# Attention with the softmax division moved behind the value product, in a 16-sequence attention and expert kernel

## The chip, the cores and the metric

The kernel runs on one core of a Trainium2 chip. The metric is the device time of one execution in microseconds; the median of three executions is taken. A core has five engines that run their own instruction lists and meet at semaphores: TensorE (PE in the profile), VectorE (DVE), ScalarE (ACT), GpSimd (POOL) and SyncE (SP, used here only to start DMAs). On-chip data lies in SBUF; TensorE writes its results to PSUM, which has 8 banks of 512 fp32 columns for each partition.

## What is computed

The input is 16 sequences of 256 tokens with 128 features. The reference, cut to its core:

```python
x = x + attention(layernorm(x))      # 16 heads of 64, 16 sequences of 256 tokens
x = x + experts(layernorm(x))        # 160 experts of 64, 8 chosen for each token, plus a shared one

# attention
dot = einsum('bihd,bkhd->bhik', q, k)
w = softmax(dot / sqrt(64), axis=-1)
a = einsum('bhij,bjhd->bihd', w, v)
return a.reshape(b, s, 1024) @ Wo + bo
```

## The kernel before

The kernel has three stages. The first does attention for all sequences, the choice of experts, and a scatter of each token's features into the slots of its 8 experts. The second does the shared expert and waits for the last scatters. The third streams the slots through the experts' weights and gathers the results. The change is in the first stage alone.

The first stage is a software pipeline. A step is one pair of heads of one sequence: 16 sequences times 8 pairs are 128 steps. In the code `b` is the sequence of the step that enters, `g` (0 to 7) its pair of heads, `step = 8 b + g`, and `u` is the step that an operation belongs to. `live(b, g, lag)` says whether the operation of step `u = step - lag` exists. Sequences 0 to 3 and the three that drain the pipeline are written out; 4 to 15 are a hardware loop over `b`. Each engine runs its own list in program order. In each step:

- TensorE does, in this order: scores of step u = step - 1 (line 379, into bank pair `psS`, three products of split fp32), queries and keys of this step (line 368, `psY`), attention output of step - 3 (line 414, `psO`, columns 0 to 255), in even `g` the values (line 368, `psVM`), transposes of the probabilities of step - 2 (line 429, `psT`, 8 blocks of 128 x 128), and the output projection of step - 4 (line 441, `psA`). Once in each sequence there are two transposes and the router's product (lines 455, 461, 499), and the ranks of the chosen experts (lines 486 to 493).
- ScalarE copies `qk_hi` (line 619), takes the exponential of the scores with their row sums in `rowsum` (line 627, four instructions in a step), copies `v_sb` in even `g` (line 633), copies the transposed probabilities of step - 2 (`probs_transposed`, line 270, two instructions), and multiplies one quarter of the probabilities of step - 1 by the inverse row sum (line 641).
- VectorE takes the row maxima (`negmax`, line 1055, two instructions), subtracts for `qk_lo` (line 1060), copies the attention output out of PSUM (`oT_sb`, line 1068), and inverts the row sums (`inverse_sums`, line 1045). Between these stands one part of the expert choice of an earlier sequence for each `g`, and the layer norms.
- GpSimd multiplies the other three quarters of the probabilities by the inverse row sums (line 768, three instructions), and then starts a part of the 16 scatters of a sequence (line 793, `SCAT`: 3 at g = 6, 4 at g = 7, 3 each at g = 0, 1 and 2). At g = 4 and 5 it has the small powers for the layer norms (lines 758 and 761) and a copy (line 755), at g = 2 the sum of the bias (line 776).

The semaphores around the change: `p_ok` counts exponentials (4 in a step), `ri_ok` inverted row sums, `pn_ok` and `pna_ok` normalised quarters on GpSimd and ScalarE, `t_ps` transposed heads (2 in a step), `pt0_ok` and `pt1_ok` their copies, `o_ps` attention outputs, `ot_ok` their copies. SyncE's DMAs of this stage wait only for counts of `s_ps`, the scores.

Of the kernel before, what the change touches and what calls it, by code (L numbers as in the profile page):

```python
# [19 lines left out]
ALU = mybir.AluOpType  # L20
ACT = mybir.ActivationFunctionType
AX = mybir.AxisListType

P = 128
B, SEQ, D = 16, 256, 128
H, DH = 16, 64
# [27 lines left out]
SCAT = [3, 4, 3, 3, 3]  # L54
# [4 lines left out]
def build(nc, x, wq, wk, wv, wo, bo, rwT, ebias, wgd, wgsT, wdsT, out):  # L59
# [4 lines left out]
    with ExitStack() as ctx:  # L64
# [36 lines left out]
        with actx:  # L101
# [80 lines left out]
            rinv = sa("rinv", [P, 2, 2, TB])  # L182
            st1 = sa("st1", [P, TB, 6])
# [35 lines left out]
        for name in """x0_in x_in wq_in wk_in wv_in c_in we_in zfill_a zfill_b yfill w_hi_ok w_lo_ok  # L219
                ln1_st ln1_ag ln1_ve ln1_rs ln1_xn xt_ps xt_hi xt_lo  # L220
                yq_ps yh_ok yl_ok v_ps v_ok s_ps nm_ok p_ok ri_ok pn_ok pna_ok t_ps pt0_ok pt1_ok o_ps ot_ok ao_ps
                xb_ok x1_ok ln2_st ln2_ag ln2_ve ln2_rs ln2_xn x2t_ps x2t_ok x2r_ok lg_ps z_ok ez_ok den_ok
                pr_ok top_ok rep_ok mask_ok rk_ps rk_cp sum_ok sm_ok s8_ok su_ok xs_ok eo_ok ti_ok eq_ok eqw_ok
                ws_ok wc_ok wi_ok wn_ok we_ok wr_ok scat
                b_ps b_dve b_pool tab_ok nbi_ok nbs_ok new_ok scan_ok fn_ok of_ok sh_ok by_ok bs_ok off_ok s1_ok mv_ok st_ok le_ok fr_ok fx_ok
                be_ok pu_ok
                w_cp xt2_ps xt2_ok g_ps h_ok y_ps y_ok
                idx_cp sh_ps hs_ok sho_ps shared_ok yw_ok ys_ok acc_ok""".split():
            s[name] = sem(name)
# [134 lines left out]
        def _(pe):  # L364
# [19 lines left out]
            def body(b):  # L384
                for g in range(G):
# [21 lines left out]
                    if live(b, g, 3):  # L407
# [3 lines left out]
                        wait(pe, s["ot_ok"], u)  # L411
                        for kt in range(TB):
# [7 lines left out]
                    if live(b, g, 2):  # L420
                        u = step - 2
                        for h in range(2):
                            wait(pe, s["pn_ok"], 3 * u + 2 + h)
                            if h == 1:
                                wait(pe, s["pna_ok"], u + 1)
# [5 lines left out]
                            m.then_inc(s["t_ps"], 1)  # L431
                    if live(b, g, 4):
# [24 lines left out]
                    if g == 6 and seq(b, 1):  # L457
# [5 lines left out]
                        m.then_inc(s["lg_ps"], 1)  # L463

# [140 lines left out]
        def _(act):  # L605
# [7 lines left out]
            def body(b):  # L613
                for g in range(G):
# [22 lines left out]
                    if live(b, g, 1):  # L637
                        u = step - 1
                        wait(act, s["ri_ok"], u + 1)
                        pq = p_sb[:, (g - 1) % 2, 1, 1, :]  # L640
                        act.activation(pq, pq, ACT.Copy, scale=rinv[:, (g - 1) % 2, 1, 1:2]).then_inc(s["pna_ok"], 1)
# [81 lines left out]
        def _(pool):  # L723
# [24 lines left out]
            def body(b):  # L748
                for g in range(G):
                    step = G * b + g  # L750
                    if g == 4 and seq(b, 2):

                        wait_apart(pool, s["mask_ok"], b - 1)
                        wait_apart(pool, s["scat"], 16 * TB * TOPK * (b - 2))
                        pool.tensor_scalar(xn2_src[:], xn2[:], 1.0, 1.0, ALU.mult, ALU.mult).then_inc(s["xs_ok"], 1)
# [6 lines left out]
                    if live(b, g, 1):  # L762

                        u = step - 1
                        wait_apart(pool, s["ri_ok"], u + 1)
                        for k in range(3):
                            pq = p_sb[:, (g - 1) % 2, k // 2, k % 2, :]
                            pool.tensor_scalar(pq, pq, rinv[:, (g - 1) % 2, k // 2, k % 2:k % 2 + 1], 1.0, ALU.mult,  # L768
                                               ALU.mult).then_inc(s["pn_ok"], 1)
# [70 lines left out]
        def _(dve):  # L840
# [198 lines left out]
            def inverse_sums(b, g, step):  # L1039
                if live(b, g, 1):  # L1040
                    u = step - 1
                    wait(dve, s["p_ok"], 4 * u + 4)
                    wait(dve, s["pn_ok"], 3 * u - 3)
                    wait(dve, s["pna_ok"], u - 1)
                    dve.reciprocal(rinv[:, (g - 1) % 2], rowsum[:, (g - 1) % 2]).then_inc(s["ri_ok"], 1)  # L1045

            def body(b):
                for g in range(G):
# [15 lines left out]
                    if live(b, g, 3):  # L1064
# [3 lines left out]
                        dve.tensor_copy(oT_sb[:, (g - 3) % 2, :], psO[:, 0, 0:SEQ]).then_inc(s["ot_ok"], 1)  # L1068
# [132 lines left out]
```

## Time and profile before

| | us |
|---|---|
| median of 3 executions | 1329.37 (1325.52 to 1330.3) |
| profiled execution, its own time | 1335.96 |
| its span in the profile | 1335.4 |
| mean granted TensorE clock, share of full | 0.844 |

In the profile a row of the view in order of time gives the start, the length, the engine, the line, the operation and the tiles, then the idle time of the engine before it and what ended it. "Remote" stands there where no record of this core explains the release. The views by stage give the busy time of each engine in a stretch; busy time of TensorE counts overlapping matmuls once.

### The profile page before, as it was taken

What the parts mean: (1) busy time and instruction counts of PE and PEld (TensorE: products, weight loads), DVE (VectorE), ACT (ScalarE), POOL (GpSimd) and SP (SyncE); (2) the same over time, 40 slices, a digit from 0 to 9 for tenths busy, and PEclk for the clock granted to TensorE, in tenths of its full rate; (3) what the DMA queues carried; (4) which work ended last, traced back from release to release, by engine and by line L of the source; (5) the groups of instructions that cost most, each with busy time, mean ns of one, the idle gap of its engine ahead of it and who ended that gap; (6) DMA issues with size and microseconds to landing.
All of it is one profiled execution on the core that took longest, in us unless ns stands there. A gap on an engine that the chain in (4) does not pass through costs nothing.

```text
span 1335.4 us, 28039 instructions
## 1 busy us (share of the span) xinstructions
PE 901.1 (67%) x7674; PEld 696.5 (52%) x7674; DVE 799.9 (60%) x2423; ACT 702.1 (53%) x2061; POOL 737.6 (55%) x989
## 2 busy tenths in 40 slices
PE   5999999988898889888985388881665556100000
PEld 4887777767777677677764156661443444100000
DVE  4579888877887788888886523330334334533332
ACT  5888777877787777777773116670433334100000
POOL 2335676667666766776676530007244444777773
PEclk9999999999999999999997659995777766555555
DMA  8604330222332233122212638882655555312211
GB/s 296 254 1 166 151 150 31 85 114 98 137 118 108 103 120 120 46 88 81 77 55 66 238 112 238 241 247 84 188 161 150 159 160 158 95 56 60 57 57 35
DMA packets 150774, 165.56 MB, mean 124 GB/s; under 512 B 13264, under 2 KB 125840, under 8 KB 150736
## 3 DMA queue, kind: packets, MB, share of 16 engines
q1 hardware_dynamic: 79440, 104.26, 22.8%
q0 software_dynamic: 16384, 33.59, 8.4%
q10 hardware_dynamic: 54912, 27.27, 7.0%
q8 instruction: 16, 0.26, 0.1%
q14 instruction: 22, 0.18, 0.0%
HBM read 64.41 MB, written 100.66 MB: 124 GB/s over the span
## 4 chain that ended last, share of the span: by engine, by line
PE 31%; issue 19%; DVE 14%; POOL 12%; another core or an unknown queue 9%; ACT 6%; DMA 6%; DVEq 1%; ACTq 1%; POOLq 0%
POOL yg L816 9%; DMA block_y<-y_b 5%; PE psS L379 5%; PE psY L368 4%; PE psO L414 4%; PE psT L429 4%; ACT p_sb L627 3%; PE psS L572 3%; PE psT L562 2%; DVE qk_lo L1060 2%; DVE negmax L1055 2%; POOL slot_x L793 2%; PE psA L441 2%; PE psY L583 2%
## 5 line engine op out<-in xcount | busy, mean ns | idle before, releaser
L816 POOL DMA_INDIRECT yg<-block_y,tok_idx x256 | 246.1, 961 | 285.0 <-DMA block_y<-y_b 149.2
L768 POOL TENSOR_SCALAR p_sb<-p_sb,rinv 128x256 f32<-128x256 f32 x384 | 189.7, 508 | 207.1 <-DVE rinv L1045 204.4
L793 POOL DMA_INDIRECT slot_x<-xn_src,slot_u x256 | 256.2, 1001 | 78.7 <-issue 77.0
L627 ACT ACTIVATE p_sb<-psS,negmax 128x256 f32<-128x256 f32 x512 | 236.4, 478 | 34.4 <-DVE negmax L1055 34.3
L1135 DVE COPY w_b<-w_all 128x192 f32 x416 | 82.8, 261 | 219.7 <-remote 88.6
L1055 DVE TENSOR_REDUCE negmax<-psS 128x2 f32<-128x512 f32 x256 | 164.1, 682 | 56.9 <-remote 27.8
L270 ACT COPY pT_sb<-psT 128x512 f32<-128x512 f32 x256 | 142.2, 616 | 33.8 <-remote 29.5
L414 PE MATMUL psO<-pT_sb,v_sb 128*64 128x256 f32 x1024 | 141.4, 397 | 24.8 <-ACT pT_sb L270 22.8
L429 PE MATMUL psT<-ident,p_sb 128*128 128x128 f32 x1024 | 139.4, 280 | 3.9 <-POOL p_sb L768 3.9
L572 PE MATMUL psS<-xbT,w_b 128*64 128x128 f32 x832 | 78.5, 316 | 78.3 <-issue 55.3
L429 PEld LDWEIGHTS psT<-ident,p_sb 128*128 128x128 f32 x1024 | 114.1, 143 | 30.9 <-issue 20.0
L619 ACT CAST qk_hi<-psY 128x512 fp32r<-128x512 f32 x128 | 74.9, 585 | 91.0 <-PE psY L368 86.7
L379 PE MATMUL psS<-qk_hi 64*128 64x256 f32 x512 | 86.6, 332 | 38.3 <-ACT p_sb L627 21.9
L627 ACT ACTIVATION_READ_ACCUMULATOR p_sb<-psS,negmax 128x1 f32 x512 | 106.9, 209 | 0.0
L1142 DVE TENSOR_TENSOR yg<-yg,wE_res 128x1024 f32<-128x1024 f32 x32 | 39.1, 1223 | 112.9 <-DMA yg<-block_y,tok_idx 112.7
L572 PEld LDWEIGHTS psS<-xbT,w_b 128*64 128x64 f32 x832 | 49.9, 153 | 101.1 <-issue 80.8
L1060 DVE TENSOR_TENSOR qk_lo<-psY,qk_hi 128x512 fp32r<-128x512 f32 x128 | 87.4, 683 | 17.5 <-ACT qk_hi L619 17.1
L414 PEld LDWEIGHTS psO<-pT_sb,v_sb 128*64 128x64 f32 x1024 | 64.3, 138 | 62.2 <-ACT pT_sb L270 23.3
L673 ACT COPY xbT<-psT 128x512 f32<-128x512 f32 x104 | 62.5, 601 | 41.5 <-remote 30.7
L679 ACT ACTIVATE h_b<-psS 128x256 f32<-128x256 f32 x104 | 40.0, 384 | 77.5 <-remote 53.4
L379 PEld LDWEIGHTS psS<-qk_hi 64*128 64x128 f32 x512 | 49.4, 187 | 59.7 <-ACT p_sb L627 28.7
L441 PE MATMUL psA<-wo_sb,oT_sb 128*128 128x128 f32 x512 | 79.4, 278 | 0.5 <-DVE oT_sb L1068 0.5
(163 smaller groups left out, 2206.6 us busy)
## 6 DMA issues: line engine op xcount, KB each, us to landing
block_y<-zero SPq DMA_DIRECT2D x26, 1024.0 KB
xb<-slot_x SPq DMA_DIRECT2D x104, 256.0 KB
block_y<-y_b ACTq DMA_DIRECT2D x104, 256.0 KB
w_all<-in_wgd_dram SPq DMA_DIRECT2D x16, 960.0 KB
slot_x<-zero SPq DMA_DIRECT2D x1, 13312.0 KB, 46.6
slot_x<-zero SPq DMA_DIRECT2D x13, 1024.0 KB
slot_x<-xn_src,slot_u POOLq DMA_INDIRECT x256
yg<-block_y,tok_idx POOLq DMA_INDIRECT x256
```

Of the source, the lines that this page charges most:

```text
L270: copy(pT_sb[:, (g - 2) % 2, h].rearrange("p a t -> p (a t)"), psT[:, h, :]).then_inc(s[f"pt{h}_ok"], 1)
L379: m = pe.matmul(psS[:, h, qt * SEQ:(qt + 1) * SEQ], a[(r, *q)], c[r, par, 1, :], start=(n == 0), stop=(n == 2))
L414: m = pe.matmul(psO[h * DH:(h + 1) * DH, 0, 0:SEQ], v_sb[:, (g - 3) // 2 % 2, kt, (g - 3) % 2, h * DH:(h + 1) * DH], pT_sb[:, (g - 3) % 2, ...
L429: m = pe.transpose(psT[:, h, kt * SEQ + qt * P:kt * SEQ + (qt + 1) * P], p_sb[:, (g - 2) % 2, h, qt, kt * P:(kt + 1) * P], ident[:])
L441: m = pe.matmul(psA[:, 0, i * P:(i + 1) * P], oT_sb[:, (g - 4) % 2, i * P:(i + 1) * P], wo_sb[:, gp, :], start=(gp == 0 and i == 0), stop= ...
L572: m = pe.matmul(psS[half, par, i // 2 * P:(i // 2 + 1) * P], w_b[:, r, i, 0:INTER], xbT[:, par, i, :], start=True, stop=True)
L627: act.activation(p_sb[:, (g - 1) % 2, h, qt, :], psS[:, h, qt * SEQ:(qt + 1) * SEQ], ACT.Exp, bias=negmax[:, (g - 1) % 2, h, qt:qt + 1], s ...
L768: pool.tensor_scalar(pq, pq, rinv[:, (g - 1) % 2, k // 2, k % 2:k % 2 + 1], 1.0, ALU.mult, ALU.mult).then_inc(s["pn_ok"], 1)
L793: pool.indirect_dma_start(slot_x, bass.IndirectOffsetOnAxis(ap=slot_u[:, i, j:j + 1], axis=0), xn2_src[:, i, :], None).then_inc(s["scat"], 16)
L816: pool.indirect_dma_start(yg[:, r, k, :], None, block_y, bass.IndirectOffsetOnAxis(ap=tok_idx[:, par, r, k:k + 1], axis=0)).then_inc(gat[r ...
L1055: dve.tensor_reduce(negmax[:, (g - 1) % 2, h, :], psS[:, h, :].rearrange("p (i k) -> p i k", i=TB), AX.X, ALU.max, negate=True).then_inc(s ...
L1060: dve.tensor_tensor(qk_lo[:, g % 2].rearrange("p a t -> p (a t)"), psY[:, 0, :], qk_hi[:, g % 2].rearrange("p a t -> p (a t)").bitcast(F32 ...
```

## The change

The probabilities stay unnormalised through the transposes and the value product. Line 768 and line 641 go. GpSimd instead spreads the four inverse row sums of a step to a tile of 128 x 256, `rinv_b`, in which each is repeated 64 times. TensorE turns it with two transposes (`row_scales`) into columns 256 to 511 of bank `psO`, ScalarE copies the result to `scale_sb`, and VectorE multiplies by it where it copied `oT_sb`. The transposes of the probabilities now wait for `p_ok`. In a step `row_scales` stands after these transposes and ahead of the output projection, and it waits for `ot_ok` of the attention output of the same step. The attention output waits for `rc_ok`, ScalarE's copy of the scales of the step before. GpSimd's copy stands first in its step, ahead of the small powers. One scatter moves from g = 7 to g = 0.

```diff
-SCAT = [3, 4, 3, 3, 3]
+SCAT = [3, 3, 4, 3, 3]
@@ tensor, attention output (live 3)
                         wait(pe, s["ot_ok"], u)
+                        wait(pe, s["rc_ok"], u + 1)
@@ tensor, transposes (live 2)
-                            wait(pe, s["pn_ok"], 3 * u + 2 + h)
-                            if h == 1:
-                                wait(pe, s["pna_ok"], u + 1)
+                            wait(pe, s["p_ok"], 4 * u + 2 + 2 * h)
...
                             m.then_inc(s["t_ps"], 1)
+                        row_scales(g, u)
@@ tensor
+            def row_scales(g, u):
+                wait(pe, s["rb_ok"], u + 1)
+                wait(pe, s["ot_ok"], u)
+                for qt in range(TB):
+                    m = pe.transpose(psO[:, 0, SEQ + qt * P:SEQ + (qt + 1) * P],
+                                     rinv_b[:, (g - 2) % 2, qt].rearrange("p h d -> p (h d)"), ident[:])
+                m.then_inc(s["r_ps"], 1)
@@ scalar, after probs_transposed
-                    if live(b, g, 1):
-                        u = step - 1
-                        wait(act, s["ri_ok"], u + 1)
-                        pq = p_sb[:, (g - 1) % 2, 1, 1, :]
-                        act.activation(pq, pq, ACT.Copy, scale=rinv[:, (g - 1) % 2, 1, 1:2]).then_inc(s["pna_ok"], 1)
+                    if live(b, g, 2):
+                        u = step - 2
+                        wait(act, s["r_ps"], u + 1)
+                        wait(act, s["ot_ok"], u)
+                        act.copy(scale_sb[:, (g - 2) % 2, :], psO[:, 0, SEQ:2 * SEQ]).then_inc(s["rc_ok"], 1)
@@ gpsimd, at the head of a step
+                    if live(b, g, 1):
+                        u = step - 1
+                        wait_apart(pool, s["ri_ok"], u + 1)
+                        wait_apart(pool, s["r_ps"], u - 1)
+                        pool.tensor_copy(rinv_b[:, (g - 1) % 2], rinv[:, (g - 1) % 2].rearrange("p h t -> p t h").unsqueeze(3)
+                                         .broadcast_to([P, TB, 2, DH])).then_inc(s["rb_ok"], 1)
@@ gpsimd, ahead of the scatters
-                        wait_apart(pool, s["ri_ok"], u + 1)
-                        for k in range(3):
-                            pq = p_sb[:, (g - 1) % 2, k // 2, k % 2, :]
-                            pool.tensor_scalar(pq, pq, rinv[:, (g - 1) % 2, k // 2, k % 2:k % 2 + 1], 1.0, ALU.mult,
-                                               ALU.mult).then_inc(s["pn_ok"], 1)
@@ vector, inverse_sums
-                    wait(dve, s["pn_ok"], 3 * u - 3)
-                    wait(dve, s["pna_ok"], u - 1)
+                    wait(dve, s["rb_ok"], u - 1)
@@ vector, attention output
+                        wait(dve, s["rc_ok"], u + 1)
-                        dve.tensor_copy(oT_sb[:, (g - 3) % 2, :], psO[:, 0, 0:SEQ]).then_inc(s["ot_ok"], 1)
+                        dve.tensor_tensor(oT_sb[:, (g - 3) % 2, :], psO[:, 0, 0:SEQ], scale_sb[:, (g - 3) % 2, :],
+                                          ALU.mult).then_inc(s["ot_ok"], 1)
```

## Rows read from the trace of the kernel before

**Rows 1.** The page: the span.

```profile
span 1335.4 us, 28039 instructions
```

**Rows 2.** Busy time by stretch: attention ahead of the scatters, and with them.

```profile
core 0: us, PE busy (x) PEld busy (x) DVE busy (x) ACT busy (x) POOL busy (x), PEclk, DMA share, GB/s
30.00:125.00 95.00, 93.21 (x819) 75.17 (x820) 69.32 (x189) 79.52 (x245) 34.44 (x68) 1.00 0.34 138
130.00:724.00 594.00, 530.23 (x4529) 421.03 (x4528) 490.87 (x1558) 439.83 (x1341) 406.36 (x585) 0.99 0.26 97
```

**Rows 3.** Waits from 130 to 724 us: who waited for whom, total, times, longest.

```profile
ACT pT_sb L270 <- remote: 29.5, 22, 2.3
DVE negmax L1055 <- remote: 27.8, 24, 1.7
PE psT L429 <- POOL p_sb L768: 3.9, 4, 2.1
```

**Rows 4.** The scatters of line 793: shortest/median/longest ns, first and last start.

```profile
L793 POOL DMA_INDIRECT slot_x<-xn_src,slot_u x256: 955/962/1253, 125.1 to 783.6; - x128
```

**Rows 5.** In order of time, VectorE at g = 3 and 4 of sequence 2, no scatters yet.

```profile
107.40 0.41 DVE L1068 COPY oT_sb<-psO 128x256 f32<-128x256 f32 x1
110.24 1.28 DVE L1055 TENSOR_REDUCE negmax<-psS 128x2 f32<-128x512 f32 x2
112.04 0.41 DVE L1068 COPY oT_sb<-psO 128x256 f32<-128x256 f32 x1
```

**Rows 6.** VectorE in the loop, one sequence apart at g = 3, with g = 4 to 2 between.

```profile
508.32 0.41 DVE L1068 COPY oT_sb<-psO 128x256 f32<-128x256 f32 x1
512.59 1.29 DVE L1055 TENSOR_REDUCE negmax<-psS 128x2 f32<-128x512 f32 x2 [1.23 <-remote]
514.39 0.41 DVE L1068 COPY oT_sb<-psO 128x256 f32<-128x256 f32 x1
530.27 0.41 DVE L1068 COPY oT_sb<-psO 128x256 f32<-128x256 f32 x1
539.00 1.29 DVE L1055 TENSOR_REDUCE negmax<-psS 128x2 f32<-128x512 f32 x2 [1.04 <-remote]
543.80 0.66 DVE L913 COPY rank_sb<-psVM 128x480 f32<-128x480 f32 x1 [1.95 <-PE psVM L493]
551.16 1.29 DVE L1055 TENSOR_REDUCE negmax<-psS 128x2 f32<-128x512 f32 x2 [0.38 <-PE psS L379]
552.97 0.41 DVE L1068 COPY oT_sb<-psO 128x256 f32<-128x256 f32 x1
```

**Rows 7.** GpSimd in the same sequence: last scatters of two groups, and what follows.

```profile
510.93 0.96 POOL L793 DMA_INDIRECT slot_x<-xn_src,slot_u  x1 [0.30 <-issue]
536.79 0.96 POOL L793 DMA_INDIRECT slot_x<-xn_src,slot_u  x1 [0.30 <-issue]
537.79 1.44 POOL L768 TENSOR_SCALAR p_sb<-p_sb,rinv 128x256 f32<-128x256 f32 x3
```

**Rows 8.** TensorE in order of time, at 62 us and at g = 7.

```profile
62.79 1.04 PE L429 MATMUL psT<-ident,p_sb 128*128 128x128 f32 x8
63.66 0.61 PE L441 MATMUL psA<-wo_sb,oT_sb 128*128 128x128 f32 x4
530.24 0.61 PE L441 MATMUL psA<-wo_sb,oT_sb 128*128 128x128 f32 x4
530.77 0.39 PE L379 MATMUL psS<-qk_hi 64*128 64x256 f32 x2
```

**Rows 9.** Like operations of other lines and the removed one, in order of time.

```profile
509.80 0.42 DVE L1084 TENSOR_TENSOR x_res<-psA,x_res 128x256 f32 x1
513.31 0.40 POOL L755 TENSOR_SCALAR xn_src<-xn 128x256 f32<-128x256 f32 x1
532.50 0.51 ACT L641 ACTIVATE p_sb<-p_sb,rinv 128x256 f32<-128x256 f32 x1
533.27 0.39 ACT L648 COPY xn2T_res<-xn2T 128x256 f32 x1
```

More of the change, by code:

```diff
@@ L182, in build @@
             rinv = sa("rinv", [P, 2, 2, TB])
+            rinv_b = sa("rinv_b", [P, 2, TB, 2, DH])
+            scale_sb = sa("scale_sb", [P, 2, SEQ])
             st1 = sa("st1", [P, TB, 6])
@@ L220, in build @@
                 ln1_st ln1_ag ln1_ve ln1_rs ln1_xn xt_ps xt_hi xt_lo
-                yq_ps yh_ok yl_ok v_ps v_ok s_ps nm_ok p_ok ri_ok pn_ok pna_ok t_ps pt0_ok pt1_ok o_ps ot_ok ao_ps
+                yq_ps yh_ok yl_ok v_ps v_ok s_ps nm_ok p_ok ri_ok rb_ok r_ps rc_ok t_ps pt0_ok pt1_ok o_ps ot_ok ao_ps
                 xb_ok x1_ok ln2_st ln2_ag ln2_ve ln2_rs ln2_xn x2t_ps x2t_ok x2r_ok lg_ps z_ok ez_ok den_ok
@@ L761, in body @@
                         pool.tensor_tensor(rs1[:], ve1[:], half[:], ALU.pow).then_inc(s["ln1_rs"], 1)
-                    if live(b, g, 1):
-                        u = step - 1
-                        wait_apart(pool, s["ri_ok"], u + 1)
-                        for k in range(3):
-                            pq = p_sb[:, (g - 1) % 2, k // 2, k % 2, :]
-                            pool.tensor_scalar(pq, pq, rinv[:, (g - 1) % 2, k // 2, k % 2:k % 2 + 1], 1.0, ALU.mult,
-                                               ALU.mult).then_inc(s["pn_ok"], 1)
                     if g == 2 and live(b, g, 0):
```

## The prediction

> **What bounds the kernel now.** I read the stages first, then the waits, then single steps in order of time. The span is 1335.4 us [rows 1]. The change touches attention alone, which ends at about 724 us, so the reader should look for what sets the pace there. It is not one thing. Until 125 us TensorE is busy for 93.2 of 95 us: it is the bound, and there is 1.8 us of room. From 130 to 724 us it is busy for 530 of 594 us, VectorE for 491, ScalarE for 440, GpSimd for 406 [rows 2]: none is full, so the pace comes from waits between them. One sequence of eight steps takes 552.97 - 508.32 = 44.65 us there [rows 6], so this stretch holds 594 / 44.65 = 13.3 sequences.
>
> The waits of that stretch are odd. VectorE's row maxima idle for 27.8 us and ScalarE's copies of the transposed probabilities for 29.5 us with no record that explains the release, while TensorE waits for GpSimd's normalised probabilities for only 3.9 us [rows 3]. So the multiplication that the change removes from GpSimd is hardly waited for itself. What is special about the stretch is the scatters, which start at 125.1 us [rows 4]. The clearest comparison is the step at g = 4. In sequence 2, ahead of any scatter, it takes 112.04 - 107.40 = 4.64 us and VectorE goes straight from the layer norm into the maxima [rows 5]. In the loop the same step takes 514.39 - 508.32 = 6.07 us, with 1.23 us of unexplained idling ahead of the maxima at 512.59 [rows 6]. A group of three scatters ends at 510.93 + 0.96 = 511.89 us, 0.70 us earlier [rows 7]. At g = 1 it is the same: 1.04 us of idling until 539.00, after a group of four scatters that ends at 536.79 + 0.96 = 537.75 us [rows 6, 7]. My reading is that TensorE's "done" signals reach the others late while a group of scatters is under way, and come through about 0.7 to 1.3 us after its end. The rows show the coincidence; they don't show the mechanism.
>
> **The change part by part.** GpSimd: three multiplications, 1.44 us [rows 7], become one copy to 128 x 256. The nearest row is its own copy of that shape, 0.40 us [rows 9]; the upper bound is the old 1.44 us, should the repeated reading be slow. I take 0.45, near the like copy. So each group of scatters starts about 1.0 us earlier, and the group at g = 7 also loses one of four scatters, about 1.27 us with its issue (0.96 + 0.30) [rows 7]. The next multiplication starts at 537.79, right as this group ends [rows 7], so GpSimd is full there and all of that comes forward: the group ends about 2.2 us earlier, at g = 0 (with one scatter more) the end is some 0.9 us earlier, at g = 2 about 1.0 to 1.4.
>
> What becomes of the unexplained idling, if it hangs on a group's end? At g = 4 the signals would come through about 1.2 us earlier, just when VectorE is ready: I take 1.0 of 1.23 us. At g = 1, VectorE no longer waits for 1.04 us; what follows is the ranks, for which VectorE waits 1.95 us until 543.80 [rows 6]. The group ahead of them has four scatters now, so I take 0.8. At g = 3 there is 0.38 us of waiting for the scores [rows 6]; I take 0.4, since it comes after the late group at g = 1 as well. Gross 2.2 us a sequence. Bounds: 0 if the idling moves along with the signals, and 3.3 if all goes (27.8 / 13.3 = 2.1 us of VectorE's remote idling [rows 3], and 1.2 of the ranks' 1.95).
>
> TensorE: two more transposes a step. Eight take 63.66 - 62.79 = 0.87 us, so two take 0.22 us [rows 8]. More important is where they stand: they wait for VectorE's `oT_sb` of the same step, and the projection and the next scores are queued behind them; VectorE, and through it ScalarE's exponentials, wait for those scores. At g = 7 VectorE ends `oT_sb` at 530.27 + 0.41 = 530.68 us [rows 6]. The two transposes add 0.22, the projection 530.77 - 530.24 = 0.53 [rows 8]: the scores start at 531.43 at the earliest, against 530.77 now, 0.66 us later. In most steps VectorE has expert work of its own to do ahead of the maxima, and covers this. Where it waits for TensorE it doesn't: I take 0.4 us at g = 7, whose scores follow a chain of such delays and the router's product, and 0.2 at g = 3. If that cover goes in all eight steps, it is 0.66 x 8. Net gain: 2.2 - 0.6 = 1.6 us a sequence, 21 us in 13.3 sequences.
>
> Ahead of the first scatter lie 22 steps in which TensorE is the bound: 22 x 0.22 = 4.8 us, less the 1.8 us of room [rows 2]: 3 us lost.
>
> ScalarE: a multiplication of 0.51 us becomes a copy of as many elements out of PSUM, nearest a copy of 0.39 us [rows 9]; between 0.39 and 0.51 this is a gain of 0 to 0.12 us a step. I count 0, since the attention output now waits for this copy (`rc_ok`) where it waited for the one ahead of it; that is hidden by the scores and the queries, which TensorE does first, except at g = 0 and 1. VectorE: the copy of 0.41 us becomes a product of PSUM and SBUF, 0.42 in a like row [rows 9]: 0.01 x 106 steps, 1 us, within the rounding. Its new wait for `rc_ok` is for a copy of the step before, which ScalarE makes ahead of the `qk_hi` that VectorE needs anyway: nothing. GpSimd's copy waits for `ri_ok` at the head of the step, and the small powers stand behind it now; they did stand ahead of the old multiplications. The inverse sums come early enough at g = 4 and 5 for this to cost 0 to 0.3 us a sequence; I take 0. The drain after the last sequence begins with three normalisations between scatters on a full GpSimd: 3 x (1.44 - 0.45) = 3 us at most, I take 2. SyncE's DMAs hang on counts of scores and come along.
>
> In the trace of before only TensorE and VectorE take turns at bank `psO`, and 0.22 + 0.53 = 0.75 us is what the new turn puts between `oT_sb` and the next scores [rows 8]. The Trainium skill, PSUM — Partial Sum Buffer, Terms, says that two engines must not use one bank and quadrant at once. By that rule TensorE, ScalarE and VectorE take turns at `psO`, so this serial cost stays as long as the scales share the bank. No row here shows a collision, and the sum is the same with the rule or without it.
>
> **The sum.** 3 - 21 - 2 = -20 us. Against the profiled execution's 1335.96 us, which is 6.6 us above the median of 1329.37, this gives 1316; against the median 1309.4.
>
> **The rivals.** First, the idling doesn't shrink but moves to other signals, and the wait for `oT_sb` decides. From the point where `oT_sb` ends later than 0.75 us ahead of the last exponential, each step loses. With 0.4 at g = 7, 0.2 at g = 3 and 0.3 each at g = 4 and 0, it is 1.2 us a sequence, 16 us, and with the 5 us of the first steps 1350 us. For it: 530.68 against 530.77. Against it: VectorE's own work covers most steps. Second, the idling goes wholly: 3.3 - 0.3 = 3.0 us a sequence, 40 us, 1289 us. For it: no such idling ahead of the scatters. Against: 256 scatters of 0.96 us remain, and each group still falls on some signal. Third, gain and loss are equal, as when the scatters' groups just trade one late signal for another at half the price: 1329, 1323 to 1335.
>
> That the idling comes from GpSimd being kept from writing its descriptors, and not from the groups' place, is part of the first rival. The scatters' durations hardly vary, 955 to 962 ns in the lower half and 1253 at most [rows 4]. The Trainium skill, SBUF — State Buffer, SBUF: two separate sides, says that a two-port VectorE operation locks GpSimd out of writing descriptors; by that rule moving the groups would free nothing and 1350 us would be the time. The durations don't bear it out.
>
> **How the numbers follow.** Forecast 0.50 (own range 1298 to 1321), slower rival 0.22, full relief 0.15, balance 0.13. The range for 8 in 10 takes in most of full relief and reaches into the slower rival: 1286 to 1345. A measurement of this kernel can tell about 0.5%, 6.6 us. Faster by more: nearly all of 0.50, and 0.15: 0.64. Slower: 0.22. The same: 0.14.
>
> **What would show it.** In the profile after: the step at g = 4 near 5 us, with little remote idling ahead of the maxima; fewer than 15 us of it over the stage; attention ending near 705 us; the ranks' wait near 1.2 us. The first 22 steps should be 3 us longer, with TensorE full. `oT_sb` should take 0.42 us. TensorE should idle ahead of the new transposes, waiting for `oT_sb`, where VectorE is late. Wrong would be: groups of scatters that end earlier while the remote idling stays at 28 us (the first rival), a GpSimd copy near 1.4 us, or a wait of the attention output for ScalarE's new copy that grows at each step.

## The result, and the profile after

The change is slower. The median of 4 executions is 1399.9 us (1398.56 to 1402.92) against 1328.03 of 4 of the kernel before: 72 us more, ratio 1.0545 (95% interval 1.0517 to 1.0573). The profiled executions differ by 66.3 us (spans 1401.7 and 1335.4).

From the page of the kernel after, the span, the busy times, and the groups of the new copy and the new transposes (line, engine, operation, tiles, count | busy, mean ns | idle time ahead of them and what ended most of it):

```profile
span 1401.7 us, 28827 instructions
PE 952.1 (68%) x7930; PEld 734.6 (52%) x7930; DVE 795.6 (57%) x2423; ACT 686.4 (49%) x2061; POOL 600.2 (43%) x733
...
L766 POOL COPY rinv_b<-rinv 128x256 f32<-128x256 f32 x128 | 53.7, 420 | 408.1 <-DVE rinv L1053 386.2
...
L472 PE MATMUL psO<-ident,rinv_b 128*128 128x128 f32 x256 | 52.1, 286 | 86.0 <-DVE oT_sb L1077 78.4
```

The prices of single operations came out as foreseen: 0.42 us for GpSimd's copy. The new cost is in the last column. TensorE stood idle for 86 us ahead of the new transposes.

The waits from 130 to 795 us of the kernel after (engine, tile and line that waited, what it waited for: us in all, times, longest):

```profile
PE psO L472 <- DVE oT_sb L1077: 75.8, 52, 2.9
...
DVE rank_sb L922 <- remote: 33.3, 10, 3.4
ACT qk_hi L630 <- remote: 32.8, 11, 3.8
...
DVE xn L869 <- POOL rs L775: 24.9, 13, 1.9
...
DVE xn L869 <- POOL rs L778: 4.4, 12, 0.4
```

And two lines of the kernel before, 130 to 724 us, to compare with:

```profile
DVE rank_sb L913 <- PE psVM L493: 31.0, 14, 4.5
...
ACT qk_hi L619 <- remote: 4.0, 1, 4.0
```

Three things stand here. The idling without a record has left the places where [rows 3] has it: the row maxima, 27.8 us before, have 2.2 us in this view, and the copies of the probabilities, 29.5 before, have 1.7. But it stands at two others now, the ranks and `qk_hi`, with 33.3 and 32.8 us. At `qk_hi` this is new. The ranks were waited for before too, for 31.0 us, but by a release that the trace shows; with 6.5 us of that kind left, their wait grew by some 9 us in all. VectorE waits for GpSimd's small powers, 13 times 1.9 us and 12 times 0.4, which it doesn't do in the kernel before. And TensorE waits for `oT_sb` 52 times.

One sequence of the loop takes 612.03 - 561.13 = 50.90 us between `oT_sb` copies, against 44.65 [rows 6]; two in a row take 612.03 - 511.70 = 100.33, so 50.2 is nearer the mean. What follows in it after the `oT_sb` of g = 4, up to that of g = 5, in order of time (start, length, engine, line, operation, then the idle time ahead of it and its releaser):

```profile
562.47 0.17 DVE L1053 RECIPROCAL rinv<-rowsum 128x4 f32<-128x4 f32 x1
562.90 0.41 POOL L766 COPY rinv_b<-rinv 128x256 f32<-128x256 f32 x1 [4.75 <-DVE rinv L1053]
563.33 0.41 POOL L772 TENSOR_SCALAR xn_src<-xn 128x256 f32<-128x256 f32 x1
563.71 0.72 POOL L775 TENSOR_TENSOR rs<-ve,half 128x2 f32<-128x2 f32 x1
564.57 0.60 DVE L869 TENSOR_SCALAR xn<-x_res,mv,rs 128x128 f32 x2 [1.93 <-POOL rs L775]
566.17 1.29 DVE L1063 TENSOR_REDUCE negmax<-psS 128x2 f32<-128x512 f32 x2
567.97 0.41 DVE L1077 TENSOR_TENSOR oT_sb<-psO,scale_sb 128x256 f32<-128x256 f32 x1
568.53 0.61 PE L472 MATMUL psO<-ident,rinv_b 128*128 128x128 f32 x2 [1.87 <-DVE oT_sb L1077]
568.95 1.06 PE L443 MATMUL psA<-wo_sb,oT_sb 128*128 128x128 f32 x4
...
571.94 0.40 PE L370 MATMUL psY<-xnT_hi,wq_hi 128*128 128x256 f32 x1
```

This is a chain through four engines that did not exist. VectorE inverts the row sums at 562.47; GpSimd, which had idled for 4.75 us, now may copy them; only then come the other copy and the power; VectorE's layer norm starts 1.93 us late, the maxima and `oT_sb` behind it are as late, and TensorE, whose next work now hangs on `oT_sb`, idles for 1.87 us. From `oT_sb` to `oT_sb` this takes 567.97 - 561.13 = 6.84 us, against 519.29 - 514.39 = 4.90 before. Here TensorE is slow afterwards as well. The granted clock of the stretch behind this idling:

```profile
core 0: us, PE busy (x) PEld busy (x) DVE busy (x) ACT busy (x) POOL busy (x), PEclk, DMA share, GB/s
...
565.00:568.00 3.00, 1.66 (x14) 1.00 (x10) 2.82 (x10) 1.43 (x6) 0.00 (x0) 1.00 0.00 0
568.00:572.00 4.00, 3.46 (x21) 2.94 (x21) 2.83 (x14) 2.07 (x7) 1.05 (x2) 0.57 0.00 0
```

It is 0.57, for the most part the lower of the two levels (1.2 of 2.4 GHz), where it was 1.00 before the idling, and the scores take 571.94 - 570.36 = 1.58 us there, against 563.65 - 562.74 = 0.91 us one step earlier. This doesn't follow each such wait: one sequence earlier, at the same place, TensorE idles even longer and the clock stays full.

```profile
519.10 0.41 PE L472 MATMUL psO<-ident,rinv_b 128*128 128x128 f32 x2 [2.13 <-DVE oT_sb L1077]
...
519.00:523.00 4.00, 3.90 (x35) 2.96 (x35) 3.46 (x14) 2.54 (x8) 1.05 (x2) 1.00 0.22 89
```

Over attention with scatters the mean granted clock is 0.97, where it was 0.99 [rows 2]. In `e14` below, which loses 62 us without scatters, it is 1.00, so the clock is not what carries the loss.

Where the 72 us lie: the last `oT_sb` of attention starts at 801.49 us instead of 724.04, 77.4 us later. The last scatter starts 73.0 us later, at 856.6 for 783.6 [rows 4]:

```profile
L802 POOL DMA_INDIRECT slot_x<-xn_src,slot_u x256: 957/962/1238, 130.1 to 856.6; - x128
```

From there to the end of the span it is 551.8 us before and 545.1 after. The change doesn't touch these stages, and another pair of profiled executions (`e9`, `e10`) has 539.4 and 547.5, so the 7 us are not a gain of the change.

### The profile page after: what moved, and what is told of

Same layout as the page of the kernel before. It is cut to its first block, busy times and chain, and to the rows that moved or that the text cites. A ratio compares the mean times of both kernels' runs of the same rounds, so it can differ in the third digit from the quotient of the medians.

```text
span 1401.7 us, 28827 instructions
## 1 busy us (share of the span) xinstructions
PE 952.1 (68%) x7930; PEld 734.6 (52%) x7930; DVE 795.6 (57%) x2423; ACT 686.4 (49%) x2061; POOL 600.2 (43%) x733
## 4 chain that ended last, share of the span: by engine, by line
PE 36%; issue 14%; DVE 13%; another core or an unknown queue 12%; POOL 11%; DMA 7%; ACT 5%; ACTq 1%; DVEq 1%; POOLq 0%
POOL yg L825 9%; DMA block_y<-y_b 7%; PE psY L370 5%; PE psS L381 5%; PE psO L417 4%; PE psT L430 4%; PE psA L443 4%; DVE qk_lo L1068 2%; PE psO L472 2%; DVE oT_sb L1077 2%; PE psS L583 2%; DVE negmax L1063 2%; PE psT L573 2%; PE psVM L370 2%
## 5 line engine op out<-in xcount | busy, mean ns | idle before, releaser
L802 POOL DMA_INDIRECT slot_x<-xn_src,slot_u x256 | 252.7, 987 | 88.1 <-issue 85.4
L766 POOL COPY rinv_b<-rinv 128x256 f32<-128x256 f32 x128 | 53.7, 420 | 408.1 <-DVE rinv L1053 386.2
L472 PE MATMUL psO<-ident,rinv_b 128*128 128x128 f32 x256 | 52.1, 286 | 86.0 <-DVE oT_sb L1077 78.4
L472 PEld LDWEIGHTS psO<-ident,rinv_b 128*128 128x128 f32 x256 | 27.9, 142 | 101.5 <-issue 100.2
## 6 DMA issues: line engine op xcount, KB each, us to landing
slot_x<-zero SPq DMA_DIRECT2D x1, 13312.0 KB, 47.3
```

Source lines behind the costliest of these rows:

```text
L472: m = pe.transpose(psO[:, 0, SEQ + qt * P:SEQ + (qt + 1) * P], rinv_b[:, (g - 2) % 2, qt].rearrange("p h d -> p (h d)"), ident[:])
L802: pool.indirect_dma_start(slot_x, bass.IndirectOffsetOnAxis(ap=slot_u[:, i, j:j + 1], axis=0), xn2_src[:, i, :], None).then_inc(s["scat"], 16)
```

## The experiments

Each edit is against the kernel named with it. Late signals, the idling that has no record, show in the traces from all chips used here but one; there (`e5` to `e8`) the kernel before takes 1211.5 us, elsewhere 1322 to 1336. So each time is given with that of the kernel before on the same chip, and ratios are against it. Where the expectations give theories a letter, A is that TensorE's wait for `oT_sb` costs the time, B that the two added transposes do, and D that the late signals and GpSimd's rhythm do. The others are told where they first come up.

**The small powers first.** In the changed kernel GpSimd's copy is moved behind them.

```diff
@@ GpSimd, body
-                    if live(b, g, 1):            # wait ri_ok, r_ps; rinv_b copy
-                        ...
                     if g == 4 and seq(b, 2):     # xn_src copy, power
 ...
                     if g == 5 and ...:           # power
 ...
+                    if live(b, g, 1):            # wait ri_ok, r_ps; rinv_b copy
+                        ...
```

> The changed kernel with one move: GpSimd's copy of the inverse row sums goes back behind the small powers and the copy at g = 4 and 5, where the old multiplications stood. Theory A (two new in-order waits: the powers queue behind the inverse sums on GpSimd, and TensorE's projection and scores queue behind the attention output's copy): VectorE's idling ahead of line 869 goes (29 us in the stage with scatters), about 1372 us, 25 to 30 below the change. Theory B (TensorE is nearly full and pays for two more transposes in each step, 128 x 0.22 = 28 us, and a pipeline that is longer): no change from 1400 us. Theory C (the groups of scatters now fall on worse signals): within 10 us of 1400.

1363.86 us against 1325.19, ratio 1.030 (1.0271 to 1.0328), where the change has 1.0545: 2.5% of the time before, some 33 us, lay in the order of two instructions in GpSimd's list. VectorE's wait for the powers is gone, and a sequence takes 47.3 us. What is left, 130 to 724 us:

```profile
PE psO L472 <- DVE oT_sb L1077: 51.2, 42, 2.6
...
DVE rank_sb L922 <- remote: 36.7, 11, 3.4
ACT qk_hi L630 <- remote: 31.0, 10, 4.2
```

**The wait alone, the transposes alone.** The first makes TensorE's wait for `ot_ok` ahead of the projection stricter by one step, so that it is for the `oT_sb` of the same step, as in the change, with nothing else; the second adds two transposes with no wait, one behind each head's four.

```diff
@@ wait alone (on the kernel before), TensorE, ahead of the projection
+                    if live(b, g, 3):
+                        wait(pe, s["ot_ok"], step - 2)
                     if live(b, g, 4):
-                        wait(pe, s["ot_ok"], u + 1)
@@ transposes alone (on the kernel before), after each head's four
+                            m = pe.transpose(psT[:, h, 0:P], p_sb[:, (g - 2) % 2, h, 0, 0:P], ident[:])
```

> The kernel before with one wait added: TensorE waits, after the transposes of a step, for VectorE's copy of the attention output of the same step, ahead of the projection; no new work. Theory A: most of the loss comes with this wait alone, 1365 us (35 to 45 us slower than before). Theory B: the wait costs nothing without the transposes, 1328 to 1333 us. Theory C: the same as B.

1324.74 us, ratio 1.0004 (0.9977 to 1.0031). TensorE does wait now, and it costs nothing that can be measured:

```profile
PE psA L442 <- DVE oT_sb L1069: 21.2, 45, 2.1
```

> The kernel before with two more transposes in each step on TensorE (one block of each head is turned twice into the same place), no new wait. Theory A: 3 us in the first 22 steps and up to 6 in the rest, 1331 to 1338 us. Theory B: 28 us, 1356 us. Theory C: 1328 us plus the first 3.

1327.85 us, ratio 1.0010 (0.9986 to 1.0034): at most 4.5 us. Both are prices over the whole run; in the first steps each of the two does cost time (see below, the first steps and the drain).

**The turn ahead of the attention output.** `row_scales` of a step goes in front of the value product instead of behind the transposes, so that it waits for `oT_sb` of the step before.

```diff
@@ changed kernel, TensorE
+                    if live(b, g, 2):
+                        row_scales(g, step - 2)
                     if live(b, g, 3):            # attention output
 ...
-                        row_scales(g, u)
@@ row_scales
-                wait(pe, s["ot_ok"], u)
+                wait(pe, s["ot_ok"], u - 1)
+                wait(pe, s["rc_ok"], u)
```

> The changed kernel with the two transposes of the inverse row sums moved: they stand behind the scores and queries of their step and ahead of its attention output, so that TensorE waits only for the attention output's copy of the step before, which is long done. ScalarE's copy still waits for that of the same step. Same work and same number of waits. Theory A: TensorE's 78 us of idling ahead of line 472 go; since part of it was shadow of VectorE's own work and the powers' delay stays, 1350 us (40 to 60 below the change). Theory B: 1400 us. Theory C: 1390 to 1410 us.

1370.91 us, ratio 1.034 (1.0311 to 1.0370): 2.1% of the time comes back. The wait for the powers stays, and TensorE waits for GpSimd's copy instead of `oT_sb`:

```profile
DVE xn L871 <- POOL rs L777: 23.0, 12, 1.9
PE psO L474 <- POOL rinv_b L768: 20.8, 14, 2.5
```

**Both moved.** The edits of `e1` and `e4` together.

> The changed kernel with both moves, the powers first and the two transposes of the inverse sums ahead of the attention output. Theory A (two in-order waits, independent): 1364 - 29 = 1335 us. Theory D (what is left after the powers is the place of the scatter groups: they now end on signals that VectorE and ScalarE are waiting for; the wait of TensorE for the attention output's copy costs nothing by itself, as the wait alone in the kernel before showed): 1350 to 1370 us, with ScalarE's and VectorE's idling without a record still there.

1199.25 us against 1211.51: ratio 0.9889 (0.9860 to 0.9919), on the chip that shows no late signals. There it beats the kernel before by 1.1%.

**Filler with the old split.** The kernel of `e1`, with two multiplications of a scratch tile on GpSimd ahead of the scatters and `SCAT` as before, to give its list the old rhythm.

```diff
@@ GpSimd, behind the rinv_b copy
+                        for k in range(2):
+                            pool.tensor_scalar(scr_out[:, k, :], scr_in[:, k, :], 1.0, 1.0, ALU.mult,
+                                               ALU.mult).then_inc(s["fl_ok"], 1)
-SCAT = [3, 3, 4, 3, 3]
+SCAT = [3, 4, 3, 3, 3]
```

> The changed kernel with the powers first, the old split of the scatters (3, 4, 3, 3, 3), and two multiplications of 128x256 on a scratch tile on GpSimd behind the copy of the inverse sums, so that the scatters start about when they did in the kernel before (1.4 us after the inverse sums). The output is whole. Theory D: the scatter groups are back at their old place, so the time falls though GpSimd does more: 1335 us, 25 to 30 below the 1364 of powers first alone. Theory A: GpSimd's extra work helps nobody, 1364 us or more.

1224.02 us, ratio 1.0090 (1.0059 to 1.0122). It ran on the chip without late signals, so it can't judge what it was made for.

**No scatters.** The 256 scatters of attention and the waits for them are left out; stage 3 reads cleared slots. First the kernel before, then the kernel of `e1`.

```diff
-                    scatter(b, g)
```

> The kernel before without the 256 scatters and without the waits for them; the slots keep their zeros, so the routed experts' part is left out of the result. It gives the pace of attention without scatters: 3.4 us less in each of 13.3 sequences (45 us), and some 45 us of the drain, 1235 us. Both theories expect this; its stretch per sequence is the base for the next one. All 24 or so stretches of idling without a record on VectorE should go.

1164.52 us, ratio 0.9603 (0.9574 to 0.9631); a sequence takes 40.46 us.

> The changed kernel with the powers first and without the scatters and the waits for them, the routed experts' part left out of the result as in the one before. Theory D: without scatters the two kernels differ only by TensorE's 0.22 us a step where it is the bound and a little more, 5 to 12 us (1240 to 1247 us against 1235), where with scatters they differ by 39. Theory A: TensorE's new waits are still there, so most of the 39 us remains: 1265 to 1275 us.

1195.32 us, ratio 0.9860 (0.9830 to 0.9891); a sequence takes 42.38 us. So 31 us of the change remain when the powers are in order and no scatter is there: the price of the turn and of GpSimd's copy, 1.92 us a sequence.

**Repeats where signals are late.** The kernel before and the change again, then the kernel before with both the wait and two transposes behind it, then both moved.

```diff
@@ wait and turn (on the kernel before), TensorE, ahead of the projection
+                    if live(b, g, 2):
+                        wait(pe, s["ot_ok"], step - 2)
+                        for qt in range(TB):
+                            pe.transpose(psO[:, 0, SEQ + qt * P:SEQ + (qt + 1) * P], ident[:], ident[:])
```

> The kernel before, unchanged, with a trace of its own beside the next three. On the chip of e5 to e8 all kernels ran some 9% shorter, and TensorE's signals came on time in every trace. If this run is on such a chip: about 1211 us, no idling without a record, and a sequence of some 43 us. If it is on one like that of the first trace: 1325 us, 44.6 us a sequence.

1324.86 against 1321.56, ratio 1.0021 (0.9991 to 1.0052).

> The changed kernel, unchanged, beside the run before. Theory A (the powers behind the inverse sums, 25 us, and the turn of the inverse sums between the attention output's copy and the next scores, 31 us as between e7 and e8): slower by 30 to 60 us on either kind of chip. Theory D (late signals): slower by 72 us where signals come late, by less than 15 where they come on time.

1399.1 us, ratio 1.0559 (1.0512 to 1.0606): the result holds on another chip.

> The kernel before with TensorE's part of the change alone: the wait for the attention output's copy of the same step and, behind it, two transposes of 128x128 (of the identity, into columns that nobody reads), ahead of the projection. GpSimd, ScalarE and VectorE are as before. The wait alone cost 0 and two transposes alone 3 us. Theory A: together they put 0.22 us between the copy and the next scores, 1.5 to 2 us a sequence, 20 to 30 us slower than before. Rival E (what costs the rest is ScalarE's new copy and the wait of the attention output for it): 0 to 6 us slower.

1334.93 us, ratio 1.0084 (1.0047 to 1.0121): 11 us. Neither part had cost it alone. It is less than theory A expected and more than E, and well below the 3.0% of `e1`, so where signals are late the turn on TensorE explains less than half of what is left after the powers. The rest must lie in what `e1` has besides: GpSimd's and ScalarE's copies, the earlier scatters and the new split.

> The kernel of e5 once more, to compare with the trace of before and of the change on the same chip. On a chip where signals come on time: 1.1% faster than before, as e5. On one where they come late: Theory A 1325 to 1340 us; Theory D 1350 to 1370 us.

1340.59 us, ratio 1.0130 (1.0084 to 1.0177). The two moves win back 4.3 of 5.6 points, but where signals are late the version stays slower than before. Its waits, 130 to 724 us:

```profile
PE psO L474 <- POOL rinv_b L779: 23.9, 15, 2.4
...
DVE rank_sb L924 <- remote: 20.8, 6, 3.5
...
DVE x_res L1096 <- remote: 13.0, 7, 1.9
```

**No scatters, where signals are late.** The kernel before and the change, both without scatters.

> The kernel of e7 (before, without scatters and their waits; the routed experts' part left out), to tell whether the late signals hang on the scatters on a chip that shows them. Where they come late, all idling without a record should go and a sequence take 40.5 us as in e7, 45 us less for attention. If the lateness is the chip's and not the scatters', it stays.

1248.48 us against 1326.98, ratio 0.9410 (0.9375 to 0.9446); 40.46 us a sequence, and no wait from 130 to 724 us is for "remote" any more.

> The changed kernel as it is, without scatters and their waits (the routed experts' part left out), beside the one before. Theory A (two in-order waits, nothing to do with scatters): the powers' 25 us and the turn's 31 us, 50 to 60 us slower than e13. Theory D (late signals make most of the 74 us): 10 to 25 us slower than e13.

1310.21 us, ratio 0.9879 (0.9847 to 0.9912): 62 us more than the run before, with no scatter. So most of the loss is not a matter of scatters or late signals. Its waits, 130 to 724 us:

```profile
PE psO L474 <- DVE oT_sb L1076: 37.3, 40, 1.8
...
DVE xn L869 <- POOL rs L776: 23.8, 13, 1.8
```

**The old split.** `SCAT` as before, in the change and in the version with both moved.

```diff
-SCAT = [3, 3, 4, 3, 3]
+SCAT = [3, 4, 3, 3, 3]
```

> The changed kernel with the old split of the scatters, 3, 4, 3, 3, 3. If the new split matters: 10 us or more off the change's 1400. Theory A: within 5 us.

1411.52 us, ratio 1.0645 (1.0611 to 1.0678), about 1 point over the change: the new split is the better one for it.

> The kernel of e5 and e12 (powers first, the turn ahead of the attention output) with the old split of the scatters. Both moved was 1.3% slower than before where signals come late and 1.1% faster where they come on time. Theory D for this rest: the split moves it by 10 us or more. Theory F (TensorE waits at the turn for GpSimd's copy, 24 us in e12, which comes from the inverse sums and not from the scatters): within 5 us of both moved.

1371.05 us, ratio 1.0318 (1.0278 to 1.0358), 1.9 points over the same version with the new split. `negmax` idles for 37.5 us with no record here, `v_sb` for 28.9: the same late signals, at other places, at another price.

**The copies left out one by one.** The scales are a constant, 0.01, set once. The first leaves out GpSimd's copy and its waits, the second ScalarE's copy and `rc_ok` too.

```diff
@@ GpSimd, body (e17 and e18, on the changed kernel)
-                        wait_apart(pool, s["ri_ok"], u + 1)
-                        wait_apart(pool, s["r_ps"], u - 1)
-                        pool.tensor_copy(rinv_b[:, (g - 1) % 2], ...).then_inc(s["rb_ok"], 1)
@@ ScalarE (e18)
-                        act.copy(scale_sb[:, (g - 2) % 2, :], psO[:, 0, SEQ:2 * SEQ]).then_inc(s["rc_ok"], 1)
```

> The change without GpSimd's copy: the scales are a constant (0.01) set once, so the inverse row sums are left out of the result; the two transposes, ScalarE's copy, its signal and VectorE's product all stay. With the copy behind the small powers the change is 3.0% over before. If the rest of that is GpSimd's share of the chain, this kernel is within 1% of before (1320 to 1340 us beside 1327). If it is the turn through TensorE and ScalarE, it stays at 1.5 to 3% over (1347 to 1367 us). The wait of the layer norm for the small powers is gone in either case.

1545.95 us against 1335.61, ratio 1.1577 (1.1551 to 1.1602). Neither reading was right: with less work the kernel became 10% slower than the change. I had overlooked that GpSimd's wait for `ri_ok`, once in each step, is also what paces the scatters, in both kernels. Without it a sequence's scatters go out in one row. From the trace in order of time, GpSimd, TensorE, ScalarE and VectorE:

```profile
359.37 1.10 POOL L796 DMA_INDIRECT slot_x<-xn_src,slot_u  x1 [3.33 <-DVE slot_u L981]
360.78 0.96 POOL L796 DMA_INDIRECT slot_x<-xn_src,slot_u  x1 [0.30 <-issue]
...
379.13 0.96 POOL L796 DMA_INDIRECT slot_x<-xn_src,slot_u  x1 [0.30 <-issue]
...
367.27 0.93 PE L463 MATMUL psVM<-rw_sb,xn2T 128*128 128x160 f32 x4 [2.89 <-issue]
...
370.94 0.41 PE L370 MATMUL psY<-xnT_hi,wk_lo 128*128 128x256 f32 x1
381.65 0.68 PE L509 MATMUL psVM<-ident,xn 128*128 128x128 f32 x2 [10.29 <-issue]
...
366.63 0.59 ACT L643 COPY v_sb<-psVM 128x512 f32<-128x512 f32 x1 [3.39 <-remote]
369.53 0.59 ACT L272 COPY pT_sb<-psT 128x512 f32<-128x512 f32 x1 [2.32 <-remote]
...
375.18 0.37 ACT L651 COPY scale_sb<-psO 128x256 f32<-128x256 f32 x1 [1.54 <-remote]
...
380.92 0.49 DVE L1103 TENSOR_TENSOR z_sb<-psVM,eb_sb 128x320 f32<-128x320 f32 x1 [15.54 <-remote]
```

TensorE ends the router's product at 367.27 + 0.93 = 368.20 us. VectorE, which waits for nothing else, takes it up at 380.92: 12.7 us later, and 0.83 us after the last of the scatters ends (379.13 + 0.96 = 380.09). The stretch before and the stretch with scatters:

```profile
345.00:359.00 14.00, 14.00 (x124) 11.24 (x122) 12.74 (x43) 11.41 (x38) 1.41 (x2) 1.00 0.19 75
359.00:381.00 22.00, 9.35 (x68) 7.31 (x64) 5.29 (x23) 5.16 (x15) 16.27 (x17) 0.78 0.27 95
```

TensorE falls from 14.00 of 14 us to 9.35 of 22. This is the clearest picture of the late signals that any run gave. They are not all held until the row has ended: ScalarE gets three of TensorE's between the scatters, at 366.63, 369.53 and 375.18, one after another and each late. The scales that it copies at 375.18 had left TensorE at 363.49 + 0.44 = 363.93, 11.3 us before (ScalarE itself was free for them from 373.64 on). The signal of the router's product comes through behind the row. In all traces of this case, from 130 to 650 us, every instruction that idles without a record waits for TensorE; `p_sb` and `qk_lo`, which read PSUM too but wait for VectorE and ScalarE, never do.

> As the run before it, and ScalarE's copy of the turned scales is left out too, with its signal: VectorE multiplies by a constant. Left are the two transposes behind the attention output of the same step, the removal of the multiplications, and the new split. If ScalarE's copy in the chain is what is still missing, this is 10 us or more below the run before it. If the wait and the transposes are, it is within 5 us of it.

1539.37 us, ratio 1.1521 (1.1485 to 1.1556), 6.6 us below the run before it, at the edge of what these runs can tell and between the two readings. As totals the two can't divide the turn's price, but their steps without scatters can. The steps by distance between `oT_sb` starts, in the loop, in us, each under the g of the copy that ends it; without scatters the kernel before has the same figures to 0.01 on both its chips (`e7`, `e13`):

| step | before, no scatters | two transposes and wait (`e18`) | with ScalarE's copy (`e17`) | with GpSimd's copy too, powers first (`e8`) | the change (`e14`) |
|---|---|---|---|---|---|
| g = 1 | 4.54 | 5.27 | 5.27 | 5.28 | 5.28 |
| g = 2 | 6.24 | 6.47 | 6.47 | 6.73 | 6.73 |
| g = 3 | 4.12 | 4.51 | 4.51 | 4.57 | 4.57 |
| g = 4 | 5.04 | 4.95 | 4.95 | 5.00 | 5.00 |
| g = 5 | 4.89 | 4.84 | 4.84 | 4.84 | 6.75 |
| sum | 24.83 | 26.04 | 26.04 | 26.42 | 28.33 |

Of the 3.50 us that the change costs in these five steps, the order of the powers is 28.33 - 26.42 = 1.91, the two transposes with the wait 26.04 - 24.83 = 1.21 (net of the multiplications that are gone), GpSimd's copy 0.38, ScalarE's copy nothing. At g = 6, 7 and 0 `e17` and `e18` have their scatters and say nothing.

## Why the prediction was wrong

The prediction took a sequence to become 1.6 us shorter: 2.2 gained from the late signals, 0.6 lost to the turn, nothing for the small powers. It became 50.2 - 44.65 = 5.5 us longer. Without scatters the powers cost 1.9 us and the turn with its copy 1.9 (`e14`, `e8`, `e7`). The scatters add 44.65 - 40.46 = 4.2 us to a sequence before and 50.2 - 44.30 = 5.9 in the change (44.30 is `e14`), so in place of a gain of 2.2 there is a loss of 1.7. All three terms were off, and two of them by more than the whole forecast.

**The small powers.** The step that failed outright reads "The inverse sums come early enough at g = 4 and 5 for this to cost 0 to 0.3 us a sequence; I take 0". The price is 1.91 us a sequence without scatters (`e14` against `e8`, at g = 5), some 33 us of the whole where signals are late (`e1`). I looked at when the inverse sums come, and not at what VectorE does next. Its list has `rinv` directly ahead of the layer norm, so a power that waits for `rinv` can't be ready: 0.41 + 0.41 + 0.72 us of GpSimd lie between. The Trainium skill, PSUM — Partial Sum Buffer, Engine vs sequencer instructions, says that the queues of ScalarE, VectorE and GpSimd are strictly first in, first out. The trace agrees: the power starts at 563.71, behind two copies, of which the first waited until 562.90; put ahead of them (`e1`), no wait of VectorE for it is left. The prediction had named what is queued behind the wait, and didn't follow who waits for that.

**The turn.** I took 0.4 us at g = 7, 0.2 at g = 3 and nothing elsewhere. Without scatters, `e8` against `e7`: 0.48 at g = 7, 0.45 at g = 3, 0.74 at g = 1, 0.49 at g = 2, and a gain of 0.19 at g = 0; in all 1.92 a sequence, three times the 0.6. The mechanism was as described, a serial piece between `oT_sb` and the next scores (with GpSimd's copy as a smaller part, 0.38 in the five steps of the table); the term was mis-sized, because "In most steps VectorE has expert work of its own to do ahead of the maxima, and covers this" was taken for g = 1 and 2 too, whose distances show that they are not covered. The bound of 0.66 x 8 would have held it. Where signals are late the wait costs nothing over the whole run (`e2`), the transposes next to nothing (`e3`) and both together 11 us (`e11`). That the idling for late signals hides the rest is likely and not shown. The slower rival, "From the point where `oT_sb` ends later than 0.75 us ahead of the last exponential, each step loses", was this, at 1350 us; it had 1.2 us a sequence for it and nothing for the powers.

**The late signals.** Half right. That they hang on the scatters is shown by `e13` (none without scatters) and `e17` (up to 12.7 us in a row of sixteen); the prediction had only the coincidence. That the row maxima would be relieved by the earlier groups came true, 27.8 us to 2.2, though their wait for the scores, with a record, grew from 8.7 to 18.8. That this is a gain of 2.2 us a sequence failed: the earlier group holds another signal. Two of them, one sequence of the kernel after:

```profile
585.75 0.96 POOL L802 DMA_INDIRECT slot_x<-xn_src,slot_u  x1 [0.31 <-issue]
...
586.82 0.59 ACT L630 CAST qk_hi<-psY 128x512 fp32r<-128x512 f32 x1 [3.13 <-remote]
...
594.35 0.96 POOL L802 DMA_INDIRECT slot_x<-xn_src,slot_u  x1 [0.30 <-issue]
...
596.39 0.66 DVE L922 COPY rank_sb<-psVM 128x480 f32<-128x480 f32 x1 [3.36 <-remote]
```

The group's last scatter ends at 586.71, `qk_hi` starts at 586.82 after 3.13 us of idling; the next ends at 595.31, the ranks are copied at 596.39 after 3.36. The lower bound of that step, "0 if the idling moves along with the signals", was nearer than the 2.2, and still too good; the first rival said it too, and so did the sign that the prediction named for it: VectorE's idling without a record went from 27.8 us to 39.7 over the stage, where fewer than 15 had been forecast. How much of the 72 us is this move can't be given as one number: the change costs 74 us with scatters (`e10` against `e9`) and 62 without (`e14` against `e13`), so scatters and late signals add some 12 by the totals, give or take 9 by their intervals, and the split alone moves the time by 1 to 1.9 points (`e15`, `e16`).

**The first steps and the drain.** The loss of 3 us ahead of the first scatter is there. `oT_sb` of g = 3 of sequence 2, at 107.40 before [rows 5], starts at 111.72, and the first scatter at 130.1 instead of 125.1 [rows 4].

```profile
111.72 0.41 DVE L1077 TENSOR_TENSOR oT_sb<-psO,scale_sb 128x256 f32<-128x256 f32 x1
```

From the first `oT_sb` to this one, 16 steps without scatters, and the loss against the kernel before:

| kernel | us | more |
|---|---|---|
| before (and `e9`) | 78.25 | |
| wait alone (`e2`) | 79.33 | 1.1 |
| two transposes alone (`e3`) | 80.71 | 2.5 |
| both (`e11`) | 81.95 | 3.7 |
| powers first (`e1`) | 81.99 | 3.7 |
| the change (and `e10`) | 82.45 | 4.2 |

Here the wait and the transposes add up, and nearly the whole loss is theirs. The reason given was not quite right: TensorE is not full, but busy for 92.1 of the 95 us from 30 to 125, where it was 93.2. The drain was to gain 2 us. Its last four steps take 801.49 - 773.90 = 27.6 us against 21.4, 6.2 more; without scatters they take 19.0 (`e14`). The row that shows why is again one of late signals, in the middle of ten scatters from 787.21 to 799.59 us that nothing paces any more:

```profile
797.21 0.66 DVE L922 COPY rank_sb<-psVM 128x480 f32<-128x480 f32 x1 [7.43 <-remote]
```

**What held.** The copy took 0.42 us for 0.45, VectorE's product 0.41 for 0.42, ScalarE's part costs nothing in the steps without scatters (`e18` against `e17`), and the idling of TensorE ahead of the new transposes was named as a thing to look for.

**What stays open.** What holds a signal of TensorE while scatters go out: no run looks inside. Why one chip doesn't show it. How the turn's price divides at g = 6, 7 and 0. What the turn costs in the steps where signals are late. And whether both moved with yet another split would beat the kernel before where signals are late: with the new split it is 1.3% over, on the other chip 1.1% under.

## What to carry to other kernels

When an instruction that waits is put ahead of others in an engine's list, follow each of those to its reader: a small operation that was always early may become the head of a chain, and it can be cheaper to turn two lines around than to save a microsecond of work. Price an added serial piece in every step, starting from its full length, and take it off only where the trace shows an idle time of the next engine that covers it. A stall that hangs on when something else runs is moved by a shift, not removed; take nothing for it until the trace shows what the shifted work will meet.

## What was unexpected of the hardware

While a row of GpSimd's indirect scatters goes out, TensorE's signals reach VectorE and ScalarE one after another and late: up to 12.7 us in one case, with sixteen scatters of 0.96 us, and TensorE itself idled for 10.3 us in it. The wait that paces the scatters is thus worth some 10% of this kernel (ratio 1.1577 without it, 1.0545 in the change that has it).

The same kernel takes 1211.5 us on one chip and 1322 to 1336 on the others, and a verdict can change its sign between them (both moved: 0.9889 and 1.0130). Without scatters attention has the same pace on both kinds, 40.46 us a sequence, the last `oT_sb` starts at 665.70 and 663.22 us, and the totals still differ (1164.5 and 1248.5): so these 84 us lie in the later stages, where the granted clock is 0.74 from 670 us to the end in `e7` and 0.69 in `e13`.

After 1.87 us of idling the granted clock of TensorE was 0.57 for the next 4 us, so this short wait was paid a second time in slow matmuls. After 2.13 us at the same place one sequence earlier it stayed at 1.00: what decides between the two no run shows.
